# Graph attention layers on one core: the factors w spread by a transfer through DRAM, instead of by TensorE products

## The chip, the cores and the metric

The kernel runs on one core of a Trainium2 chip. The metric is the device time of one execution in microseconds (us); of several runs the median is taken. The engines are named as in the profile: PE is TensorE, DVE VectorE, ACT ScalarE, POOL GpSimd, SP SyncE, whose queue issues the transfers.

## The reference, cut to what matters

There are 64 graphs of 128 nodes with 384 features, and a 128 x 128 mask for each. Layer 0 is attention with 6 heads of 64, layer 1 graph attention with 12 heads of 32; both end in a residual sum and a layer norm. The change is in layer 1's weights:

```
h = einsum('bnd,ade->bane', feat_in, W);  th = tanh(h)
attn_src = einsum('bane,aeo->bano', th, w_src)
attn_dst = einsum('bane,aeo->bano', th, w_dst)
attn = attn_src + swapaxes(attn_dst, 2, 3)
attn = where(attn >= 0, attn, 0.2 * attn)
attn = softmax(where(~adj, -999.0, attn), axis=-1)
feat_out = einsum('banm,bame->bane', attn, h) + b
...
return gate * elu(feat_out) + (1.0 - gate) * feat_in
```

## The kernel before, in words

Work goes by groups of 4 graphs, 16 groups in all. Layer 1 of group u, layer 0 of group u+1 and the transposes of x for group u+2 are interleaved. Every engine has its program as a list of steps (name, graph or part k), in three tables: BEGIN, LOOP and END. LOOP is run 13 times as it stands, one pass per group. `phases` walks the tables, and `step` issues what a name stands for; so the order on each engine is fixed by hand-written tables, and semaphores make a step wait where its data or its buffer isn't there. Most buffers are doubled (k % 2). The products of 384 or 512 columns are made of three times three fp32r products of high and low parts (`project`, L573): ACT writes the high part (x1hi), DVE the low one (x1lo, L910).

In layer 1, the exponential of leaky(src_i + dst_j), divided by exp(src_i) (which the softmax cancels), is max(p_j, q_j w_i) with p = exp(dst), q = exp(0.2 dst), w = exp(-0.8 src). Node j lies on the partitions, i along them. The steps for one graph are:

- `h` (PE), `hout` (ACT, th at L836), `prod` (POOL, L1132), `sd`, `sda`, `wlog` (DVE, L1001 to L1012), then `pqw` (ACT): p, q and w as 128 x 12 each.
- `qwhi` and `qwlo` split q and w into parts (L866, L910), `qwT` transposes them (PE, L703) and `qwTo` copies them (ACT, L873).
- `rows` (POOL, L1139) lays w out as 96 x 1536 rows with zeros where the head is another's. `wb` (PE, three per graph, L712) multiplies: each gives q_j w_i for 4 heads as 128 x 512 in a PSUM bank, t_bank, of which there are two, shared with all transposes.
- `e` (DVE, L1032), three per graph with four instructions each, forms the weights of one head: the maximum with p_j and the minimum with clip, which holds the mask.
- `pv1` (PE, L726 and L732) sums values and denominators, `sumsTo`, `sumsT`, `rden1`, `f_raw`, `fb`, `elu`, `ex`, `mixa`, `mixb`, `sum1`, `stats1`, `mv1`, `rstd1` and `out` make y_out.

SP's program is short: per pass it issues the load of x_in and adj_in (`load`) and four stores. `maskT` and `clip` prepare the mask, `gate` and `gsum` the gate (L995), `x_res` (POOL, L1115) the residual with the biases.

## Time and profile before

| | us |
|---|---|
| median of 3 runs (1105.11 to 1106.05) | 1105.98 |
| profiled execution, its own time | 1105.45 |
| profiled execution, span | 1103.6 |
| PE busy | 1056.6 (96%) |
| DVE busy | 872.9 (79%) |
| POOL busy | 703.9 (64%) |
| ACT busy | 651.4 (59%) |

The busy shares are of the span. A pass of the loop repeats every 65.8 us from about 127 us on, 13 times. The drain (the last 120 us or so) holds what is left of the last two groups.

### The profile page before, as it was taken

The page shows a single profiled execution, that of the slowest core. Times are in us where ns is not written, and L with a number is a line of the kernel's source. Part 1 is how long each engine was busy: PE and PEld are TensorE (multiplying, and loading weights), DVE is VectorE, ACT ScalarE, POOL GpSimd, SP SyncE. Part 2 cuts the span into 40 slices and gives each one's busy share as a digit, 9 for nine tenths or more (in the row PEclk, how much of TensorE's full clock was granted, in tenths as well). Part 3 has the DMA queues.
Part 4 walks back from the last instruction along what each step waited for, and adds up shares of the span by engine and source line. Part 5 has one row for each costly group of instructions (what it writes and reads, how often), then busy time and mean ns, then how long its engine had stood idle before and what let it go on. Part 6 is the DMA issues. An engine that isn't in the chain of part 4 may idle for free.

```text
span 1103.6 us, 28424 instructions
## 1 busy us (share of the span) xinstructions
PE 1056.6 (96%) x9199; PEld 895.9 (81%) x9199; DVE 872.9 (79%) x2289; ACT 651.4 (59%) x2060; POOL 703.9 (64%) x605
## 2 busy tenths in 40 slices
PE   6999999999999999999999999999999999999964
PEld 4888888888888888888888888888888888888753
DVE  3659779696987969789696987969689796978986
ACT  4747466474755647565575746657565564747522
POOL 0347577575757758577574856757576674857764
PEclk9999999999999999999999999999999999999985
DMA  7101010010101001010100101001010100100000
...
DMA packets 34722, 31.00 MB, mean 28 GB/s; under 512 B 15872, under 2 KB 34688, under 8 KB 34688
## 3 DMA queue, kind: packets, MB, share of 16 engines
...
q14 instruction: 15, 0.12, 0.0%
...
## 4 chain that ended last, share of the span: by engine, by line
PE 79%; DVE 12%; issue 6%; ACT 1%; POOL 0%; DMA 0%; DVEq 0%; POOLq 0%; ACTq 0%
PE p_bank L573 50%; PE t_bank L712 5%; PE context L726 5%; DVE weights L1032 4%; PE scores L635 4%; PE context L732 4%; PE t_bank L644 3%; PE context L656 3%; PE t_bank L605 2%; PE t_bank L740 2%; PE t_bank L682 2%; DVE sd L1001 1%; DVE masked L940 1%; DVE neg_max L948 1%; PE t_bank L703 1%
## 5 line engine op out<-in xcount | busy, mean ns | idle before, releaser
L1139 POOL TENSOR_TENSOR w_rows<-qwT,own_head 96x1536 fp32r<-96x1536 f32 x64 | 179.8, 2810 | 87.0 <-ACT qwT L873 87.0
L1032 DVE SCALAR_TENSOR_TENSOR weights<-t_bank,pqw,clip 128x128 f32<-128x128 f32 x768 | 206.4, 344 | 7.4 <-PE t_bank L712 6.6
L1132 POOL TENSOR_TENSOR prod<-th,w_sd 128x768 f32<-128x768 f32 x64 | 118.2, 1846 | 124.8 <-ACT th L836 124.7
L808 ACT ACTIVATE probs<-masked,neg_max 128x128 f32<-128x128 f32 x384 | 148.8, 391 | 46.4 <-DVE neg_max L948 46.4
L573 PE MATMUL p_bank<-xT,w_q 128*128 128x512 f32 x432 | 113.6, 408 | 4.3 <-DVE w_k L917 4.3
L573 PE MATMUL p_bank<-w_v,xT 128*128 128x384 f32 x576 | 115.2, 344 | 1.2 <-DVE clip L985 1.2
L573 PE MATMUL p_bank<-w_f,cT 128*128 128x384 f32 x576 | 115.4, 344 | 0.4 <-DVE cT L910 0.4
L573 PE MATMUL p_bank<-w_h,x1T 128*128 128x384 f32 x576 | 114.0, 343 | 0.2 <-DVE x1T L910 0.2
L573 PE MATMUL p_bank<-w_g,x1T 128*128 128x384 f32 x576 | 113.9, 342 | 0.0
L573 PE MATMUL p_bank<-xT,w_k 128*128 128x512 f32 x432 | 111.5, 402 | 0.0
L1120 POOL TENSOR_TENSOR probs<-probs,rden 128x768 f32<-128x768 f32 x64 | 94.3, 1473 | 25.2 <-DVE rden L953 25.2
L573 PEld LDWEIGHTS p_bank<-w_h,x1T 128*128 128x128 f32 x576 | 101.7, 190 | 6.2 <-issue 2.6
L573 PEld LDWEIGHTS p_bank<-w_v,xT 128*128 128x128 f32 x576 | 99.7, 188 | 5.6 <-issue 3.6
L573 PEld LDWEIGHTS p_bank<-w_g,x1T 128*128 128x128 f32 x576 | 101.9, 190 | 2.1
L573 PEld LDWEIGHTS p_bank<-w_f,cT 128*128 128x128 f32 x576 | 99.1, 188 | 1.7 <-DVE cT L910 1.0
L573 PEld LDWEIGHTS p_bank<-xT,w_q 128*128 128x128 f32 x432 | 80.2, 191 | 24.4 <-DVE w_k L917 4.7
L1144 POOL TENSOR_TENSOR f_b<-f_raw,bias 128x384 f32<-128x384 f32 x64 | 71.3, 1113 | 42.0 <-DVE f_raw L1047 42.0
L1150 POOL TENSOR_TENSOR elu_steps<-elu_steps,x 128x384 f32<-128x384 f32 x64 | 75.0, 1172 | 31.0 <-ACT elu_steps L884 25.5
L1001 DVE TENSOR_REDUCE sd<-prod 128x24 f32<-128x768 f32 x64 | 60.4, 944 | 41.7 <-POOL prod L1132 41.7
L573 PEld LDWEIGHTS p_bank<-xT,w_k 128*128 128x128 f32 x432 | 79.5, 190 | 16.2
L712 PE MATMUL t_bank<-w_rows,qwT 96*128 96x512 f32 x192 | 84.1, 465 | 6.3 <-ACT probs0T L817 2.1
L995 DVE TENSOR_TENSOR gate_sum<-p_bank,gate_bias 128x384 f32<-128x384 f32 x64 | 35.1, 548 | 64.1 <-PE p_bank L573 64.0
...
## 6 DMA issues: line engine op xcount, KB each, us to landing
x_in<-in_x_dram SPq DMA_DIRECT2D x16, 768.0 KB, 4.7
out_dram<-y_out SPq DMA_DIRECT2D x64, 192.0 KB, 1.9
...
x<-in_L_gnn_W_dram SPq DMA_DIRECT2D x3, 192.0 KB, 6.1
```

What stands on the lines that cost most here:

```text
L573: last = te.matmul(dst, left(a, kt), right(b, kt), start=(n == 0), stop=(n == 3 * KT - 1))
L635: last = te.matmul(scores[:, b, j * P:(j + 1) * P], head(qT, j, b, k), head(kT, j, b, k), start=True, stop=True)
L712: te.matmul(dst[:, :], qwT[:, g % 2, 0, :], w_rows[0:QW_ROWS, g % 2, heads, :].rearrange("p h i -> p (h i)"), start=True, stop=True).then_ ...
L726: te.matmul(context1[t * HD1:(t + 1) * HD1, r * P:(r + 1) * P], h[:, k % 2, n * HD1:(n + 1) * HD1], weights[:, k % 2, n, :], start=(r == 0 ...
L808: last = act.activation(probs0[:, k % 2, b, j * P:(j + 1) * P], masked[:, k % 2, b * PAIRS + j, :], ACT.Exp, bias=neg_max[:, b * PAIRS + j ...
L1001: dve.tensor_reduce(sd[:].rearrange("p a h -> p (a h)"), prod[:].rearrange("p a (h e) -> p (a h) e", h=H1), AX_X, ALU.add).then_inc(s_sd, 1)
L1032: last = dve.scalar_tensor_tensor(out=weights[:, g % 2, n, :], in0=src[:, i * P:(i + 1) * P], scalar=pqw[:, g % 2, 0, n:n + 1], in1=clip[: ...
L1120: pool.tensor_tensor(probs, probs, per_head(rden0[:], P), ALU.mult).then_inc(s_norm, 1)
L1132: pool.tensor_tensor(prod[:], over_heads(th[:], 2), w_sd[:], ALU.mult).then_inc(s_prod, 1)
L1139: pool.tensor_tensor(w_rows[0:QW_ROWS, k % 2], over_heads(qwT[:, k % 2, 1, :].bitcast(F32), H1), per_head(own_head[:], P), ALU.mult).then_ ...
L1144: pool.tensor_tensor(f_b[:, k % 2, :].rearrange("p (h e) -> p h e", h=H1), f_raw[:].rearrange("p (h e) -> p h e", h=H1), over_heads(bias_1 ...
L1150: pool.tensor_tensor(exp_less_x, f_exp, x1[:, k, :], ALU.subtract).then_inc(s_ex, 1)
```

## The change

The products of w and q leave PE. Per graph:

- ACT's `pqw` writes p and q to a tile pq, and w to w_exp (128 x 12). `qwhi`, `qwlo`, `qwT`, `qwTo` and `wb` are gone, with their tiles.
- SP has two new steps. `keep` waits for w and writes it to a DRAM scratch w_kept (128 rows of 48 bytes). `spread` waits for that, and for the maxima that read the buffer two graphs before, and reads the 1536 numbers back to every partition: w_spread[:, k % 2] as [i, head], 768 KB.
- `rows` (POOL) now multiplies w_spread by q in place, 128 x 1536.
- `e` (DVE) reads head n of w_spread, every twelfth word, in place of a PSUM bank.
- SP now has tables of its own, and the tables of the four engines are new throughout.

The diff without the tables (one line of one table stands for them):

```diff
 PE_LOOP = [
-    ("v", 0), ("x1T", 0), ("qk", 0), ("x1T", 1), ("qk", 1), ("qk", 2), ("h", 0), ("gate", 0), ("qk", 3), ("h", 1),
+    ("qk", 0), ("qk", 1), ("x1T", 0), ("v", 0), ("qk", 2), ("x1T", 1), ("h", 0), ("gate", 0), ("x1T", 2), ("qk", 3),
...
+SP_LOOP = [
+    ("keep", 0), ("spread", 0), ("load", 0), ("keep", 1), ("spread", 1), ("keep", 2), ("spread", 2), ("keep", 3),
+    ("spread", 3), ("store", 0), ("store", 1), ("store", 2), ("store", 3),
+]
...
-        pqw = sb("pqw", [P, 2, 3, H1])
-        qw_parts = sb("qw_parts", [P, 2, 2, QW_ROWS], F32R)
-        qwT = sb("qwT", [QW_ROWS, 2, 2, P], F32R)
-        own_head = sb("own_head", [QW_ROWS, H1])
-        w_rows = sb("w_rows", [P, 2, H1, P], F32R)
+        pq = sb("pq", [P, 2, 2, H1])
+        w_exp = sb("w_exp", [P, 2, H1])
+        w_kept = [nc.dram_tensor(f"w_kept{i}", [P, H1], F32, kind="Internal").ap() for i in range(2)]
+        w_spread = sb("w_spread", [P, 2, P, H1])
...
+                elif name == "keep":
+                    sp.wait_ge(s_pqw, upto(g1, 3 * GROUP, 3 * k + 3))
...
+                    wait(sp, s_wspread[k % 2], upto(g1, GROUP // 2 * 16, k // 2 * 16))
...
+                    sp.dma_start(w_kept[k % 2], w_exp[:, k % 2, :]).then_inc(s_kept[k % 2], 16)
+                elif name == "spread":
+                    sp.wait_ge(s_kept[k % 2], upto(g1, GROUP // 2 * 16, (k // 2 + 1) * 16))
...
+                    wait(sp, s_e, upto(g1, THIRDS * GROUP, THIRDS * (k - 1)))
...
+                    sp.dma_start(w_spread[:, k % 2].rearrange("p i h -> p (i h)"),
+                                 w_kept[k % 2].rearrange("i h -> (i h)").partition_broadcast(P)
+                                 ).then_inc(s_wspread[k % 2], 16)
...
-                    te.matmul(dst[:, :], qwT[:, g % 2, 0, :],
-                              w_rows[0:QW_ROWS, g % 2, heads, :].rearrange("p h i -> p (h i)"),
-                              start=True, stop=True).then_inc(pe["wb"], 1)
...
+                    act.activation(w_exp[:, k % 2, :], wlog[:], ACT.Exp, scale=LEAKY - 1.0).then_inc(s_pqw, 1)
...
                     for i in range(H1 // THIRDS):
                         n = H1 // THIRDS * r + i
-                        last = dve.scalar_tensor_tensor(out=weights[:, g % 2, n, :], in0=src[:, i * P:(i + 1) * P],
-                                                        scalar=pqw[:, g % 2, 0, n:n + 1], in1=clip[:, g, :],
+                        last = dve.scalar_tensor_tensor(out=weights[:, g % 2, n, :], in0=w_spread[:, g % 2, :, n],
+                                                        scalar=pq[:, g % 2, 0, n:n + 1], in1=clip[:, g, :],
                                                         op0=ALU.max, op1=ALU.min)
...
                 elif name == "rows":
-                    pool.wait_ge(s_qwT, upto(g1, GROUP, k + 1))
...
-                    pool.tensor_tensor(w_rows[0:QW_ROWS, k % 2], over_heads(qwT[:, k % 2, 1, :].bitcast(F32), H1),
-                                       per_head(own_head[:], P), ALU.mult).then_inc(s_rows, 1)
+                    pool.wait_ge(s_wspread[k % 2], upto(g1, GROUP // 2 * 16, (k // 2 + 1) * 16))
+                    pool.wait_ge(s_pqw, upto(g1, 3 * GROUP, 3 * k + 2))
+                    pool.tensor_tensor(w_spread[:, k % 2], w_spread[:, k % 2], over_heads(pq[:, k % 2, 1, :], P),
+                                       ALU.mult).then_inc(s_prod1, 1)
```

How the tables move instructions is shown at three places. The first is PE in the loop, from the product of w_h with x1T of graph 0 on (names: w_h gives h, w_g the gate, w_q and w_k queries and keys). Before, and then in the change:

```order
L573 MATMUL p_bank<-w_h,x1T 128x384 x9
L463 REGISTER_ALU
L573 MATMUL p_bank<-w_g,x1T 128x384 x9
L573 MATMUL p_bank<-xT,w_k 128x512 x9
L573 MATMUL p_bank<-w_h,x1T 128x384 x9
L703 MATMUL t_bank<-ident,qw_parts 96x128 x2
L463 REGISTER_ALU
L573 MATMUL p_bank<-xT,w_q 128x512 x9
L679 REGISTER_ALU
L682 MATMUL t_bank<-ident,x 128x128 x3
```

```order
L582 MATMUL p_bank<-w_h,x1T 128x384 x9
L461 REGISTER_ALU
L582 MATMUL p_bank<-w_g,x1T 128x384 x9
L691 MATMUL t_bank<-ident,x 128x128 x3
L582 MATMUL p_bank<-xT,w_k 128x512 x9
L582 MATMUL p_bank<-w_h,x1T 128x384 x9
L461 REGISTER_ALU
L582 MATMUL p_bank<-xT,w_q 128x512 x9
L582 MATMUL p_bank<-xT,w_k 128x512 x9
L461 REGISTER_ALU
L582 MATMUL p_bank<-w_g,x1T 128x384 x9
```

Behind the gate of graph 0 there now stand the transposes of x1 for graph 2 and one product of 512 columns before h of graph 1, and two products of 512 columns before the gate of graph 1. The transposes of qw_parts are gone.

The second is DVE in the loop, at the maximum-minimum instructions of graph 0 (weights; masked and neg_max belong to layer 0 of the next group). Before, and then in the change:

```order
L948 TENSOR_REDUCE neg_max<-masked 128x6
L1022 REGISTER_ALU
L1032 SCALAR_TENSOR_TENSOR weights<-t_bank,pqw,clip 128x128 x8
L935 REGISTER_ALU
L940 TENSOR_TENSOR masked<-scores,neg 128x768
L1022 REGISTER_ALU
L1032 SCALAR_TENSOR_TENSOR weights<-t_bank,pqw,clip 128x128 x4
L1022 REGISTER_ALU
L1032 SCALAR_TENSOR_TENSOR weights<-t_bank,pqw,clip 128x128 x4
L1022 REGISTER_ALU
L1032 SCALAR_TENSOR_TENSOR weights<-t_bank,pqw,clip 128x128 x4
L953 RECIPROCAL rden<-den 128x6
```

```order
L910 REGISTER_ALU
L915 TENSOR_TENSOR masked<-scores,neg 128x768
L993 ISA
L461 REGISTER_ALU
L1000 SCALAR_TENSOR_TENSOR weights<-w_spread,pq,clip 128x128 x12
L923 TENSOR_REDUCE neg_max<-masked 128x6
L970 TENSOR_TENSOR gate_sum<-p_bank,gate_bias 128x384
L976 TENSOR_REDUCE sd<-prod 128x24
L928 RECIPROCAL rden<-den 128x6
L461 REGISTER_ALU
L983 TENSOR_TENSOR sda<-sd,sd_shift 128x24
L1000 SCALAR_TENSOR_TENSOR weights<-w_spread,pq,clip 128x128 x4
```

The twelve of graph 0 stood in pieces between two other steps, each waiting for a PSUM bank; now they stand in one piece after the second masked, and those of graph 1 follow after the sums sd of graph 2.

The third is SP in the loop, from its first DMA on. Before, and then in the change:

```order
L511 ISA
L511 DMA x_in<-in_x_dram 128x4x384
L512 REGISTER_ALU
L512 DMA adj_in<-in_adj_dram 128x4x128
L517 ISA
L518 ISA
L518 DMA out_dram<-y_out 128x384
L517 REGISTER_ALU
L518 ISA
L518 DMA out_dram<-y_out 128x384
```

```order
L520 DMA w_kept<-w_exp 128x12
L523 REGISTER_ALU
L461 REGISTER_ALU
L528 DMA w_spread<-w_kept 128x1536
L507 ISA
L511 ISA
L511 DMA x_in<-in_x_dram 128x4x384
L512 REGISTER_ALU
L512 DMA adj_in<-in_adj_dram 128x4x128
L515 REGISTER_ALU
L520 DMA w_kept<-w_exp 128x12
L528 DMA w_spread<-w_kept 128x1536
```

The load of x_in and adj_in now stands between the spread of graph 0 and the keep of graph 1; the stores follow behind the spread of graph 3.

## Rows read from the trace of the kernel before

**Rows 1.** The page: the span, then busy us (share) and instructions.

```profile
span 1103.6 us, 28424 instructions
...
PE 1056.6 (96%) x9199; PEld 895.9 (81%) x9199; DVE 872.9 (79%) x2289; ACT 651.4 (59%) x2060; POOL 703.9 (64%) x605
```

**Rows 2.** Windows: busy us in one middle pass and in the drain.

```profile
core 0: us, PE busy (x) PEld busy (x) DVE busy (x) ACT busy (x) POOL busy (x), PEclk, DMA share, GB/s
...
521.90:587.70 65.80, 65.11 (x575) 55.30 (x575) 53.66 (x143) 40.20 (x129) 44.00 (x38) 1.00 0.08 25
979.90:1103.60 123.70, 98.18 (x862) 81.37 (x861) 96.24 (x254) 55.73 (x176) 76.33 (x66) 0.88 0.05 19
```

**Rows 3.** PE in the middle pass: start us, us, instructions.

```profile
525.96 1.72 PE L573 MATMUL p_bank<-w_h,x1T 128*128 128x384 f32 x9
...
529.08 2.27 PE L573 MATMUL p_bank<-xT,w_k 128*128 128x512 f32 x9
...
532.81 0.42 PE L703 MATMUL t_bank<-ident,qw_parts 128*96 128x128 f32 x2
533.17 2.38 PE L573 MATMUL p_bank<-xT,w_q 128*128 128x512 f32 x9
...
542.77 0.39 PE L712 MATMUL t_bank<-w_rows,qwT 96*128 96x512 f32 x1
543.09 0.94 PE L635 MATMUL scores<-kT,qT 64*128 64x128 f32 x12
```

**Rows 4.** DVE in the same pass, same columns; in brackets the wait before.

```profile
524.14 0.56 DVE L910 TENSOR_TENSOR x1T<-t_bank,x1T 128x384 fp32r<-128x384 f32 x1
529.28 0.56 DVE L995 TENSOR_TENSOR gate_sum<-p_bank,gate_bias 128x384 f32<-128x384 f32 x1 [4.58 <-PE p_bank L573]
...
530.33 0.94 DVE L1001 TENSOR_REDUCE sd<-prod 128x24 f32<-128x768 f32 x1
...
542.62 0.94 DVE L948 TENSOR_REDUCE neg_max<-masked 128x6 f32<-128x768 f32 x1
543.48 2.15 DVE L1032 SCALAR_TENSOR_TENSOR weights<-t_bank,pqw,clip 128x128 f32<-128x128 f32 x8
...
546.40 3.19 DVE L1032 SCALAR_TENSOR_TENSOR weights<-t_bank,pqw,clip 128x128 f32<-128x128 f32 x12
549.50 0.19 DVE L953 RECIPROCAL rden<-den 128x6 f32<-128x6 f32 x1
...
577.85 0.55 DVE L1054 SCALAR_TENSOR_TENSOR mix<-f_b,elu_steps 128x384 f32<-128x384 f32 x1
578.31 0.23 DVE L1040 RECIPROCAL rden<-t_bank 128x12 f32<-128x12 f32 x1
```

**Rows 5.** Groups by line: busy us, mean ns | idle before, releaser.

```profile
L1132 POOL TENSOR_TENSOR prod<-th,w_sd 128x768 f32<-128x768 f32 x64 | 118.2, 1846 | 124.8 <-ACT th L836 124.7
...
L1115 POOL TENSOR_TENSOR x_res<-x_in,out_bias 128x1536 f32<-128x1536 f32 x16 | 56.0, 3499 | 28.2 <-DVE out_bias L925 28.2
...
L836 ACT ACTIVATE th<-p_bank 128x384 f32<-128x384 f32 x64 | 30.8, 481 | 19.0 <-PE p_bank L573 18.9
...
L910 DVE TENSOR_TENSOR qw_parts<-pqw,qw_parts 128x24 fp32r<-128x24 f32 x64 | 12.3, 193 | 26.9 <-ACT qw_parts L866 26.8
```

**Rows 6.** DMA issues of the page: count, KB each, median us to landing.

```profile
x_in<-in_x_dram SPq DMA_DIRECT2D x16, 768.0 KB, 4.7
out_dram<-y_out SPq DMA_DIRECT2D x64, 192.0 KB, 1.9
```

**Rows 7.** POOL in the middle pass, in order of time.

```profile
569.86 1.01 POOL L1150 TENSOR_TENSOR elu_steps<-elu_steps,x 128x384 f32<-128x384 f32 x1
...
575.85 1.63 POOL L1150 TENSOR_TENSOR elu_steps<-elu_steps,x 128x384 f32<-128x384 f32 x1 [1.34 <-ACT elu_steps L884]
```

**Rows 8.** PE in the drain, in order of time.

```profile
1062.58 0.90 PE L740 MATMUL t_bank<-ident,sumsT 128*128 128x128 f32 x4 [2.85 <-ACT sumsT L843]
...
1066.28 3.08 PE L573 MATMUL p_bank<-w_h,x1T 128*128 128x384 f32 x9
```

More of the change, by code:

```diff
@@ L187 @@
-    ("stats1", 2, 1), ("mixa", 3, 1), ("mixb", 3, 1), ("mv1", 2, 1), ("sum1", 3, 1), ("stats1", 3, 1), ("mv1", 3, 1),
-    ("out", 2, 1), ("out", 3, 1),
+    ("x1lo", 0, 0), ("gsum", 0, 0), ("x1lo", 1, 0), ("sd", 0, 0), ("sda", 0, 0), ("wlog", 0, 0), ("sd", 1, 0),
+    ("sda", 1, 0), ("wlog", 1, 0), ("gsum", 1, 0), ("x1lo", 2, 0), ("mask", 0, 0), ("max", 0, 0), ("e", 0, 0),
+    ("e", 1, 0), ("e", 2, 0), ("mask", 1, 0), ("rden0", 0, 0), ("max", 1, 0), ("x1lo", 3, 0), ("e", 3, 0),
+    ("e", 4, 0), ("e", 5, 0), ("sd", 2, 0), ("sda", 2, 0), ("wlog", 2, 0), ("rden1", 0, 0), ("f_raw", 0, 0),
@@ L217 @@
-ENGINES = ("PE", "ACT", "DVE", "POOL")
+    ("x_res", 0, 0), ("prod", 0, 0), ("prod", 1, 0), ("rows", 0, 0), ("rows", 1, 0), ("norm", 0, 0), ("prod", 2, 0),
+    ("fb", 0, 0), ("prod", 3, 0), ("norm", 1, 0), ("norm", 2, 0), ("ex", 0, 0), ("rows", 2, 0), ("norm", 3, 0),
+    ("fb", 1, 0), ("rstd0", 0, 0), ("ex", 1, 0), ("rows", 3, 0), ("rstd0", 1, 0), ("fb", 2, 0), ("prod", 0, 1),
+    ("rstd1", 0, 0), ("ex", 2, 0), ("prod", 1, 1), ("rstd0", 2, 0), ("rstd1", 1, 0), ("fb", 3, 0), ("rstd0", 3, 0),
@@ new lines @@
+    ("ex", 3, 0), ("rows", 0, 1), ("prod", 2, 1), ("rows", 1, 1), ("prod", 3, 1), ("rstd1", 2, 0), ("fb", 0, 1),
+    ("ex", 0, 1), ("rows", 2, 1), ("rstd1", 3, 0), ("rows", 3, 1), ("fb", 1, 1), ("ex", 1, 1), ("fb", 2, 1),
+    ("rstd1", 0, 1), ("ex", 2, 1), ("fb", 3, 1), ("rstd1", 1, 1), ("ex", 3, 1), ("rstd1", 2, 1), ("rstd1", 3, 1),
+]
+SP_BEGIN = [
+    ("load", 0, -1), ("keep", 0, 0), ("spread", 0, 0), ("keep", 1, 0), ("spread", 1, 0), ("keep", 2, 0),
+    ("load", 0, 0), ("spread", 2, 0), ("keep", 3, 0), ("spread", 3, 0), ("store", 0, 0), ("store", 1, 0),
+    ("store", 2, 0), ("store", 3, 0),
+]
@@ L218 @@
+ENGINES = ("PE", "ACT", "DVE", "POOL", "SP")
 ORDERS = {
-    "begin": dict(zip(ENGINES, (PE_BEGIN, ACT_BEGIN, DVE_BEGIN, POOL_BEGIN))),
+    "begin": dict(zip(ENGINES, (PE_BEGIN, ACT_BEGIN, DVE_BEGIN, POOL_BEGIN, SP_BEGIN))),
     "loop": {e: [(name, k, 0) for name, k in steps]
-             for e, steps in zip(ENGINES, (PE_LOOP, ACT_LOOP, DVE_LOOP, POOL_LOOP))},
-    "end": dict(zip(ENGINES, (PE_END, ACT_END, DVE_END, POOL_END))),
+             for e, steps in zip(ENGINES, (PE_LOOP, ACT_LOOP, DVE_LOOP, POOL_LOOP, SP_LOOP))},
+    "end": dict(zip(ENGINES, (PE_END, ACT_END, DVE_END, POOL_END, SP_END))),
@@ L514, in store @@
-            def store(t):
-                for g in range(GROUP):
-                    graph = at(t * GROUP + g)
-                    sp.wait_ge(s_y, upto(t, GROUP, g + 1))
-                    sp.dma_start(out_dram[:, bass.ds(graph, 1), :],
-                                 y_out[:, g % 2, :].unsqueeze(1)).then_inc(s_store[g % 2], 16)
-            load(1)
-            load(2)
-            store(0)
-            with sp.Fori(1, NG - 2) as u:
-                load(u + 2)
-                store(u)
@@ L529, in _ @@
+            phases(sp, step, "SP", NG)
             for g in range(2):
@@ L1155, in _ @@
             phases(pool, step, "POOL", NG)
-T_STAGES = {"sumsT", "pT", "qwT", "xT", "x1T", "wb", "maskT"}
+T_STAGES = {"sumsT", "pT", "xT", "x1T", "maskT"}
 P_STAGES = {"qk", "v", "f", "h", "gate"}
```

262 lines of the change are left out of this document (104 added, 158 removed), and 119 rows, old and new, of tables (DVE_BEGIN, DVE_END, DVE_LOOP, PE_BEGIN).

## The prediction

> **What bounds the kernel now.** I read the page's busy shares first, then the busy time of one pass of the loop, then PE's and DVE's instructions in that pass in order of time. It gives PE 96%, DVE 79%, POOL 64%, ACT 59% [rows 1]. These are means over start, 13 equal passes and drain, so the pass decides. In a middle pass of 65.80 us PE is busy 65.11 us at a granted clock of 1.00 (the 2.4 GHz level), DVE 53.66, POOL 44.00, ACT 40.20 [rows 2]. PE is the bound, but the other number to find is how far behind it DVE stands. DVE waits 65.80 - 53.66 = 12.1 us per pass. The first wait is the telling one: DVE makes the low part of x1T of a group's first graph at 524.14 (done 524.70), and the product that needs it starts on PE only at 525.96 [rows 3, 4]. So PE is ahead of DVE's need by 1.3 us, and all the rest of DVE's waiting, 10.8 us, is time in which DVE waits for work that it has itself let loose: DVE's own chain would give a pass of about 64.5 us. **There are two bounds, 65.8 and 64.5**, and a change that relieves PE alone is cut off 1.3 us down.
>
> **PE, relieved.** Out go 12 products t_bank<-w_rows,qwT and 4 pairs of transposes of qw_parts per pass. Their busy times overlap with their neighbours', so I take start to start: 542.77 to 543.09 is 0.32 us for a product, 532.81 to 533.17 is 0.36 for a pair [rows 3]. (12 x 0.32) + (4 x 0.36) = 5.3 us; PE's bound becomes 65.8 - 5.3 = 60.5 us.
>
> **ACT.** Three small copies per graph go from an engine that idles 25.6 us of the pass [rows 2]: nothing.
>
> **DVE, the term that decides.** Four small subtractions on qw_parts (193 ns each [rows 5], some 0.13 start to start) go: -0.5 us. The 48 maximum-minimum instructions stay, but their first operand moves from PSUM, 128 adjacent words, to SBUF, 128 words 12 apart (w_spread is laid out [i, head], and head n is read). Now: 12 of them from 546.40 to 549.50 are 0.258 us each [rows 4]. Without a price for the hop: two SBUF operands of 384 take 0.46 us start to start (577.85 to 578.31), and 768 read once take 0.86 (542.62 to 543.48), so a word costs 0.40/384 = 1.04 ns and 128 cost 0.46 - 256 x 1.04 ns = 0.19 us. No row shows DVE hopping. Bounds: hops free, 0.19 us (48 x -0.065 = -3.1 us); or as slow per word as the slowest elementwise row of the trace, GpSimd's x_res, 3499/1536 = 2.28 ns [rows 5], so 0.19 + 128 x 1.24 ns = 0.35 us (+4.5 us). I take twice the contiguous pace, 0.19 + 0.133 = 0.326 us (+3.3 us): every DVE row that fits 1.04 ns walks neighbours, and a walk that never uses a word's neighbour should not keep that pace. It is a choice, nearer to the upper end. DVE's work is then 53.66 - 0.5 + 3.3 = 56.5 us.
>
> The Trainium skill (Vector Engine (DVE) Microarchitecture Reference, section on rate slope and fixed cost, the SBUF access granule) says that a DVE port keeps its full rate only on runs of two or more adjacent words; it gives 1.73 ns per column for one source that hops far at every word, and 2.50 for both sources stepping 24 words. No run here shows it yet. By 1.73 the term would be +1.1 us, by 2.50 +5.9 us.
>
> **DVE's waits in the new order.** From the moment x1lo of graph 0 is done: PE runs h and gate, 525.96 to 529.08 [rows 3], so gate_sum starts 3.3 us later: a 3.3 us wait. gate_sum and x1lo 1 (529.28 to 530.33), sd, sda and wlog 0 (1.45 us) bring DVE to 5.8. Its next step, sd 1, needs h 1, which in the new PE order stands behind x1T 2 and one product of 512 columns: 3.12 + 0.25 + 2.1 + 1.7 = 7.2 (the 512 columns by the third row of [rows 3], 2.27 less the 0.16 that overlaps), then th 0.5 and prod 1.85 [rows 5], so 9.8: a wait of 4.0. sd, sda, wlog 1 to 11.25; gate 1 behind two more products of 512 columns ends at 13.1: 1.9. gate_sum, x1lo 2, masked 0, max 0 to 16.0; scores 1 ends at 16.4: 0.5. Sum 9.7 us that no speed of DVE shortens. Behind it DVE has 39 us of work in one stretch, where waits of POOL and ACT hardly show once DVE is the slow one: 0.5. **The pass is 56.5 + 9.7 + 0.5 = 66.7 us**, 0.9 more than now, with PE waiting 6 us in it.
>
> **The new transfer.** For the first graph: w_exp is ready 6.3 us after x1lo 0; a store of y_out lands in 1.9 us and an x_in of the same 768 KB as the spread in 4.7 [rows 6]; the product in place is x_res's case (1536 words, one operand repeated), 3.5 us. 6.3 + 1.9 + 4.7 + 3.5 = 16.4, and the first maximum-minimum stands at 17.4 (after masked 1). Hidden, with 1.0 us to spare. SP waits in the keep and in the spread; behind them stand the load, needed some 30 us later, and the stores, needed in the next pass: nothing. The bytes, 64 x 768 KB = 50 MB, are small beside idle queues (DMA share 0.08 [rows 2]). POOL's instruction stays one of 1536 words, and POOL idles 21.8 us of a pass [rows 2]: its length matters only where DVE waits for it. A GpSimd step can stretch, though: exp_less_x took 1.01 us beside maximum-minimum reading PSUM (569.86) and 1.63 beside DVE work on two SBUF operands (575.85) [rows 7]; the new one reads two SBUF operands, so the in-place product of graph 1 may take up to 5.6 instead of 3.5 us. It ends at 24 to 26 against DVE's need at 24: within the 0.5.
>
> The Trainium skill (GPSIMD Engine Reference, key points) names the contention of GpSimd with DVE instructions that have two SBUF inputs; these two rows agree with it (1.01 and 1.63 us).
>
> **Start and drain** hold three more groups. PE's saving there is up to 3 x 5.3 = 16 us where it bounds (at the start), DVE's loss 3 x 3.3 = 10 where that does (the last 123.7 us: DVE 96.2, PE 98.2 us busy at 0.88 [rows 2]); and the first and last chains are longer: 1.9 + 4.7 + 3.5 against about 4.6 us for copies, transposes, rows and product, +5.5 each. I take +3, between -10 and +11. **Sum:** the profiled execution took 1105.45 us (span 1103.6); 1105.5 + 13 x 0.9 + 3 = 1120.2. The median of the runs is 0.5 above it: 1121 us.
>
> **Rivals.** Hops are free (the other side: faster). The term is -3.1, DVE's work 50.1; the in-place products of graphs 1 and 3 and the exp chain then end 1 to 1.5 us after DVE is ready for each, 3.5 in all: 50.1 + 9.7 + 3.5 = 63.3, so 1105.5 - 13 x 2.5 - 3 = 1070. It decides at a start-to-start time below about 0.27 us. For it: DVE's writes of rden 4 words apart cost nothing that shows. Against: that is 12 words.
>
> Near steps cost more than twice. At a price above the GpSimd row, 0.38 us, the pass is 69.3 and the time 1105.5 + 46 + 6 = 1157. For it speaks no row, against it that not even GpSimd, at 2.28, is that slow on neighbours.
>
> The sentence of the Trainium skill's Vector Engine (DVE) Microarchitecture Reference on two sources at 24 words, 2.50 ns, is a rule that would bring this case about; our step is 12 words, on one source.
>
> The round trip is slow. If the 48-byte packets of the keep and the 128 reads of one row make it 3.2 us longer, the spare 1.0 is gone and each pass waits 2.2 us more at its first maximum-minimum, behind which all of DVE is queued: 1121 + 29 = 1150. For: no row shows packets of 48 bytes, nor one row read by all partitions in a quiet stretch; against: the two kinds shown agree with a small fixed time and 768 KB in 3 us more.
>
> PE's clock falls in the new wait. In a pass of 66.7 us PE has some 6 us to wait, and the order puts most of it at one place, before h of graph 0, behind DVE's x1lo. In the drain, after a wait of 2.85 us with little work around it, the nine products of w_h took 3.08 us instead of 1.72 (1.2 GHz, the granted clock 0.88 over the drain [rows 2, 8]). If each pass does the same, h and gate of graph 0 cost 3.1 us more, right on DVE's chain: 1121 + 13 x 3.1 = 1161. For: the drain; against: the drain has several waits in a row, here there is one in 66 us.
>
> PE stays the bound, which is what the counts of the diff alone suggest: 1105.5 - 13 x 5.3 = 1037, less if start and drain gain too. It needs DVE's 10 us of waits to vanish; the new order keeps them.
>
> **How the numbers follow.** Forecast (0.27 to 0.35 us per instruction, 1098 to 1135) 0.34; free hops 0.22; dearer hops 0.18; clock 0.12; slow round trip 0.08; PE bound 0.06. A measurement can tell 0.2%, some 2.2 us. Faster: 0.22 + 0.06 + 0.07 from the forecast's low edge = 0.35; same 0.06; slower 0.59. The range reaches down to take in free hops with their ends (1066), and up to the dear hops and the slow trip with half of the clock's case (1160).
>
> **What would show it.** Right: in a middle pass PE busy near 60 us of 66 to 67, DVE's long stretch without gaps, the maximum-minimum at 0.33 us start to start. Wrong: 0.19 to 0.25 there; or waits of DVE for w_spread's product at the first one; or transfers above 6 us. A pass near 60.5 would overturn the account of two bounds.

## The result, and the profile after

The changed kernel takes **1479.34 us** (median of 4 runs, 1476.95 to 1480.76), the kernel before in the same session 1105.55 us (1102.65 to 1106.05). The ratio is 1.3386, 95% interval 1.3355 to 1.3417: slower by a third. The forecast said slower, at 1121 us, and its range ended at 1160. The sign was right and the size was off by a factor of 24 (+374 us for +15.5). The terms that made it "slower" in the forecast come to 15 us, and the larger part of the 374 comes from one that stood there at next to nothing; so the right sign is in good part luck.

The page of the changed kernel, against [rows 1]:

```profile
span 1476.5 us, 27475 instructions
...
PE 1105.7 (75%) x8879; PEld 943.4 (64%) x8879; DVE 1221.2 (83%) x2225; ACT 611.3 (41%) x1868; POOL 749.6 (51%) x600
```

DVE has 64 instructions fewer than before and is busy 348 us longer (1221.2 against 872.9). That is nearly all of the loss, and the trace books it as *busy* time, not as idle time: something made DVE's instructions last. Two passes of the loop in the middle, against [rows 2] (windows: from:to, length, busy us of each engine, clock, DMA share, GB/s):

```profile
642.61:733.80 91.19, 69.65 (x554) 59.43 (x554) 76.17 (x139) 37.54 (x116) 46.60 (x37) 0.85 0.15 53
733.80:823.58 89.78, 68.44 (x554) 58.77 (x554) 76.07 (x139) 37.53 (x116) 46.69 (x37) 0.89 0.16 54
```

A pass went from 65.8 to 90.5 us, DVE in it from 53.7 to 76.1. Next the groups by line (mean ns of one behind the comma), for which [rows 5] stand; before, y_out had a mean of 483 ns, the first mix 551, the last sum 565:

```profile
L1000 DVE SCALAR_TENSOR_TENSOR weights<-w_spread,pq,clip 128x128 f32<-128x128 f32 x768 | 503.7, 722 | 3.7 <-POOL w_spread L1099 3.7
L1099 POOL TENSOR_TENSOR w_spread<-w_spread,pq 128x1536 f32<-128x1536 f32 x64 | 222.8, 3481 | 37.3 <-DMA w_spread<-w_kept 37.3
...
L1046 DVE TENSOR_SCALAR y_out<-sum,mv,rstd 128x384 f32<-128x384 f32 x64 | 74.9, 1170 | 1.7 <-POOL rstd L1065 0.7
...
L1022 DVE SCALAR_TENSOR_TENSOR mix<-f_b,elu_steps 128x384 f32<-128x384 f32 x64 | 54.4, 850 | 4.3 <-POOL elu_steps L1110 4.3
...
L1033 DVE SCALAR_TENSOR_TENSOR sum<-mix,x 128x384 f32<-128x384 f32 x64 | 46.8, 732 | 0.6
```

The maximum-minimum (called e below) has a mean of 722 ns, for 344 before. A mean hides what kind of loss it is, so the next view is the one line's own spread (minimum/median/maximum in ns), before and then in the change:

```profile
L1032 DVE SCALAR_TENSOR_TENSOR weights<-t_bank,pqw,clip x768: 311/343/354, 72.6 to 1086.0; 128x128 f32<-128x128 f32 x192
...
L1000 DVE SCALAR_TENSOR_TENSOR weights<-w_spread,pq,clip x768: 392/431/3522, 74.2 to 1460.0; 128x128 f32<-128x128 f32 x192
```

Median 431 ns, maximum 3522. So most of them pay a little (the hop, that is, the read of words 12 apart), and some take eight times the median. Before, none took over 354 ns. Where do the long ones stand? DVE's instructions in a stretch of the pass, in order of time (start us, us):

```profile
712.31 8.79 DVE L1000 SCALAR_TENSOR_TENSOR weights<-w_spread,pq,clip 128x128 f32<-128x128 f32 x12
...
746.99 7.64 DVE L1000 SCALAR_TENSOR_TENSOR weights<-w_spread,pq,clip 128x128 f32<-128x128 f32 x8
...
759.56 1.48 DVE L1000 SCALAR_TENSOR_TENSOR weights<-w_spread,pq,clip 128x128 f32<-128x128 f32 x4
760.95 0.56 DVE L1015 TENSOR_TENSOR f_raw<-t_bank,rden 128x384 f32<-128x384 f32 x1
...
778.78 3.60 DVE L1046 TENSOR_SCALAR y_out<-sum,mv,rstd 128x384 f32<-128x384 f32 x1
```

and POOL's in the same stretch:

```profile
713.90 1.91 POOL L1094 TENSOR_TENSOR prod<-th,w_sd 128x768 f32<-128x768 f32 x1 [2.61 <-ACT th L828]
715.77 3.46 POOL L1099 TENSOR_TENSOR w_spread<-w_spread,pq 128x1536 f32<-128x1536 f32 x1
...
747.14 1.52 POOL L1082 TENSOR_TENSOR probs<-probs,rden 128x768 f32<-128x768 f32 x1 [1.42 <-DVE rden L928]
748.63 1.03 POOL L1110 TENSOR_TENSOR elu_steps<-elu_steps,x 128x384 f32<-128x384 f32 x1
749.63 3.46 POOL L1099 TENSOR_TENSOR w_spread<-w_spread,pq 128x1536 f32<-128x1536 f32 x1
...
778.70 3.47 POOL L1077 TENSOR_TENSOR x_res<-x_in,out_bias 128x1536 f32<-128x1536 f32 x1
```

Where POOL idles, at 759.56, four e take 760.95 - 759.56 = 1.39 us, 0.35 each. Twelve e beside prod and the w_spread product take 8.79 us, which is 12 x 0.35 = 4.2 and another 4.6. And y_out, 0.08 us after x_res began, lasts until 0.21 us after x_res ended. The DVE instruction does not run slowly; it is held until the end of POOL's. All 172 e that last over 830 ns end 0.16 to 0.17 us after the end of a POOL instruction. That is less than an e's own 0.39, so it is let go a little before the end that is recorded for POOL.

Of 768 e 428 met no POOL instruction (longest 461 ns), 340 did (median 960; an overlap of over 50 ns counts). Before, 721 of the 768 lay beside a POOL instruction, and none lasted over 354 ns. In the changed kernel itself the lines of DVE that read PSUM, and the reductions and statistics with their one operand, keep their time too: gate_sum lasts 559 ns at most (median 550) with 38 of 64 beside POOL, the stats of layer 1 582 (550) with 49 of 64. Summed over all, e's time above its median is 228 us, of which 94 at the w_spread product and the rest at prod, probs, f_b and elu_steps; the rise of the median by 88 ns makes another 68. By the busy time of each group, e grew by 297 us (206.4 to 503.7), y_out by 44, mix by 19, sum by 11 and the x of layer 0 by 11 (475 to 626 ns); qw_parts' 12 us are gone, and sda, 24 words, lost 20 (533 to 218 ns). Together 350 us, against DVE's 348.

**Theories at this point.** Theory 1: an e that reads two buffers of SBUF and a POOL instruction exclude each other; before, e's first operand lay in PSUM. Theory 2: the read 12 words apart is the cost. Theory 3: the transfer through DRAM and the new orders make the passes long. DVE's idle time speaks against a large share of it: span less busy time is 231 us before and 255 in the changed kernel.

### The profile page after: what moved, and what is told of

Its sections match the earlier page's. It is cut to its first block, busy times and chain, and to the rows that moved or that the text cites. A ratio compares the mean times of both kernels' runs of the same rounds, so it can differ in the third digit from the quotient of the medians.

```text
span 1476.5 us, 27475 instructions
## 1 busy us (share of the span) xinstructions
PE 1105.7 (75%) x8879; PEld 943.4 (64%) x8879; DVE 1221.2 (83%) x2225; ACT 611.3 (41%) x1868; POOL 749.6 (51%) x600
## 4 chain that ended last, share of the span: by engine, by line
DVE 32%; issue 29%; PE 27%; POOL 9%; ACT 1%; DMA 1%; DVEq 1%; POOLq 0%; ACTq 0%; SPq 0%
PE p_bank L582 18%; DVE weights L1000 17%; POOL w_spread L1099 3%; PE context L718 2%; POOL prod L1094 2%; DVE mix L1022 2%; PE context L724 2%; PE scores L644 2%; DVE sum L1033 2%; PE t_bank L732 1%; POOL f_b L1104 1%; DVE sd L976 1%; DVE f_raw L1015 1%; DVE stats L1037 1%; PE t_bank L653 1%
## 5 line engine op out<-in xcount | busy, mean ns | idle before, releaser
L1000 DVE SCALAR_TENSOR_TENSOR weights<-w_spread,pq,clip 128x128 f32<-128x128 f32 x768 | 503.7, 722 | 3.7 <-POOL w_spread L1099 3.7
L718 PE MATMUL context<-weights,h 128*32 128x128 f32 x1536 | 108.8, 367 | 256.2 <-DVE weights L1000 256.2
L1099 POOL TENSOR_TENSOR w_spread<-w_spread,pq 128x1536 f32<-128x1536 f32 x64 | 222.8, 3481 | 37.3 <-DMA w_spread<-w_kept 37.3
L718 PEld LDWEIGHTS context<-weights,h 128*32 128x32 f32 x1536 | 55.6, 143 | 275.5 <-DVE weights L1000 272.8
L582 PE MATMUL p_bank<-w_h,x1T 128*128 128x384 f32 x576 | 134.9, 386 | 46.9 <-DVE x1T L885 46.5
L582 PE MATMUL p_bank<-w_g,x1T 128*128 128x384 f32 x576 | 129.2, 375 | 4.2 <-DVE gate_sum L970 4.2
L582 PEld LDWEIGHTS p_bank<-w_g,x1T 128*128 128x128 f32 x576 | 115.3, 215 | 7.8 <-issue 4.9
L830 ACT ACTIVATE h<-p_bank 128x384 f32<-128x384 f32 x64 | 31.2, 488 | 208.0 <-PE context L724 208.0
L724 PE MATMUL context<-weights,one_hot 128*32 128x128 f32 x1536 | 110.4, 372 | 0.0
L835 ACT ACTIVATE sumsT<-context 128x512 f32<-128x512 f32 x64 | 38.0, 593 | 150.3 <-PE context L724 150.3
```

Of the source, the lines that this page charges most:

```text
L582: last = te.matmul(dst, left(a, kt), right(b, kt), start=(n == 0), stop=(n == 3 * KT - 1))
L718: te.matmul(context1[t * HD1:(t + 1) * HD1, r * P:(r + 1) * P], h[:, k % 2, n * HD1:(n + 1) * HD1], weights[:, k % 2, n, :], start=(r == 0 ...
L724: last = te.matmul(context1[t * HD1:(t + 1) * HD1, D:D + P], one_hot[:, r, :], weights[:, k % 2, n, :], start=False, stop=(r == THIRDS - 1))
L835: act.activation(sumsT[:], context1[:, :], ACT.Copy).then_inc(s_sumsT, 1)
L1000: last = dve.scalar_tensor_tensor(out=weights[:, g % 2, n, :], in0=w_spread[:, g % 2, :, n], scalar=pq[:, g % 2, 0, n:n + 1], in1=clip[:, ...
L1099: pool.tensor_tensor(w_spread[:, k % 2], w_spread[:, k % 2], over_heads(pq[:, k % 2, 1, :], P), ALU.mult).then_inc(s_prod1, 1)
```

## The experiments

Where no ratio is given, the time is that of a single execution. The kernel before took 1106.45 us beside adjacent, pool_short, one_operand and old_adjacent, 1104.3 (median) beside adj_short, old_hop, split4 and act_spread, and 1105.1 beside one_short, act_adjacent and fold_act; its times spread by 0.5%.

### One part of the new operand at a time

**e reads adjacent words** (label adjacent):

```diff
- in0=w_spread[:, g % 2, :, n],
+ in0=w_spread[:, g % 2].rearrange("p i h -> p (i h)")[:, n * P:(n + 1) * P],
```

> The changed kernel with one edit: the weights step e reads 128 adjacent words of w_spread in place of 128 words 12 apart. The pairs' factors are then the wrong ones (left out: that word (i, h) goes with pair (i, h)); the amount of work of every instruction is the same. Theory 1 (two buffers of SBUF: a VectorE instruction whose two data operands both lie in SBUF does not finish while a GpSimd instruction runs; it waits that one out): only the hop's price goes, about 0.15 us x 48 = 7 us in a pass of 90.5, so about 1380 us, and some of the e instructions beside w_spread still last 1 to 3.5 us. Theory 2 (the read 12 apart is itself what costs, by a cost that varies with what else reads SBUF): e falls to 0.19 to 0.26 us for all, and the kernel to about 1110 us. Theory 3 (the transfer and the new orders make the passes long, not e): within 30 us of 1479.

Measured: 1403.47 us, 76 less than the changed kernel, where theory 1 had said about 1380.

```profile
L1000 DVE SCALAR_TENSOR_TENSOR weights<-w_spread,pq,clip x768: 300/342/3568, 75.6 to 1385.0; 128x128 f32<-128x128 f32 x192
```

The median falls from 431 to 342 ns, what it was with PSUM (343), and the maximum stays. The hop costs 89 ns of 128 words, 0.70 ns a word, the same for each. Theory 2 asked for 1110: it falls. The hop is a part (76 us), and not the large one. Theory 1's value was too low since it took the hop at 150 ns.

**POOL's product cut to 12 words** (label pool_short):

```diff
- pool.tensor_tensor(w_spread[:, k % 2], w_spread[:, k % 2], over_heads(pq[:, k % 2, 1, :], P),
+ pool.tensor_tensor(w_spread[:, k % 2, 0:1], w_spread[:, k % 2, 0:1], over_heads(pq[:, k % 2, 1, :], 1),
```

> The changed kernel with one edit: GpSimd multiplies 12 of the 1536 words of each partition of w_spread by q (left out: q in the other 1524, so layer 1's weights lack q). Every other instruction, buffer and wait stays. Theory 1 (VectorE waits out a running GpSimd instruction): GpSimd's 3.48 us x 4 per pass go, and with them the e that last up to 3.5 us; what is left are x_res and prod, so 13 to 20 us less per pass, 1200 to 1310 us. Theory 2 (the read 12 apart costs by itself): e stays at 0.72 us mean, and the kernel within 20 us of 1479, since GpSimd was at work only half of the time. Theory 3 (the transfer is late): the product leaves the path from the transfer to e, 3.4 us sooner per group, at most 7 us per pass: not under 1390.

Measured: 1356.95 us, 122 less. e itself is untouched, POOL was idle half of the time, and DVE's e are busy 93 us less (410.6 for 503.7). Their longest is now 1930 ns, a prod long, where it was a w_spread product long. The effect was smaller than my 1200 to 1310: of the 228 us only the 94 at the product are gone, and the 133 at prod, probs (`norm` in the tables), f_b and elu_steps are still there, 133 us.

**Both together** (label adj_short):

> The changed kernel with two of the edits of the first batch together: e reads 128 adjacent words, and GpSimd multiplies 12 words of each partition (left out: q in the others, and the right pairing of w's words). Alone they gave 1403 (-76) and 1357 (-122). If they are one loss counted twice (an e that is shorter meets fewer GpSimd instructions, and fewer GpSimd instructions leave less to meet), the two together give less than their sum: 1290 to 1320. If they add up as independent costs: 1281. What then remains over 1106 is e beside prod, norm and x_res, and y_out beside x_res: by the kernel before with a plain SBUF operand (1307) not below 1250.

Measured: 1297.82 us, -182 for -76 and -122: a little less than the sum, and in the range for one loss that is partly counted twice. What remains over the kernel before is 193 us, with a plain read and hardly a product.

**e with one SBUF operand** (label one_operand):

```diff
- last = dve.scalar_tensor_tensor(out=weights[:, g % 2, n, :], in0=w_spread[:, g % 2, :, n],
-                                 scalar=pq[:, g % 2, 0, n:n + 1], in1=clip[:, g, :],
-                                 op0=ALU.max, op1=ALU.min)
+ last = dve.tensor_reduce(weights[:, g % 2, n, :], w_spread[:, g % 2, :, n:n + 1], AX_X, ALU.max)
```

> The changed kernel with one edit: e becomes a VectorE reduction over one element with the same 128 words 12 apart read and the same 128 bf16 written, so it reads one SBUF buffer, not two (left out: the max with p and the min with the clip; layer 1's weights are w q alone, also where there is no edge). GpSimd's product stays whole. Theory 1 (two SBUF buffers are what makes it wait for GpSimd): no e lasts over 0.5 us, beside w_spread or not, and the e part of the loss (about 235 of 373 us) goes: 1200 to 1270 us, y_out and mix still stretched. Theory 2 (the read 12 apart costs by itself): unchanged, 1479 within 30. Theory 3 (transfer and orders): unchanged.

Measured: 1241.65 us, 238 less, with the hop, the transfer, the long product and all orders in place.

```profile
L1000 DVE TENSOR_REDUCE weights<-w_spread x768: 296/375/406, 75.5 to 1223.5; 128x128 f32<-128x128 f32 x192
```

None is over 406 ns, though 532 of the 768 now lie beside a POOL instruction. So neither the hop nor the buffer that POOL works on too makes an e wait. The edit also changes the kind of instruction, so that it is the second operand in SBUF rests on this run together with old_adjacent below, which changes nothing but the place of an operand. The profile shows at once who is next in the queue. The first mix, with two SBUF operands, now meets the products and goes from 850 to

```profile
L1020 DVE SCALAR_TENSOR_TENSOR mix<-f_b,elu_steps 128x384 f32<-128x384 f32 x64 | 96.7, 1511 | 4.2 <-POOL elu_steps L1108 4.2
```

**That and the short product** (label one_short), for the 136 us which that kernel still has over the one before:

> The changed kernel with two edits of the first batch together: e is a reduction with one SBUF operand, and GpSimd multiplies 12 words per partition (left out: the max with p, the min with the clip, and q in most words). Alone they gave 1242 and 1357. Theory 1: with the one e meets nobody, so what is left of 136 us over the kernel before is mix, sum and y_out beside GpSimd; without the 3.48 us products mix falls from 1.51 back to 0.7 us and sum stays at 0.6 to 0.76, which is 50 to 60 us less: 1175 to 1200 us, y_out beside x_res (45 us) being left. If instead the 136 us are the new orders and the way through DRAM, the product's length matters little: 1225 to 1242 us.

Measured: 1175.91 us, 66 less, at the lower edge. Left are 71 us, and DVE is busy 69 us longer than before (942.0 for 872.9): y_out beside x_res (1170 for 483 ns, 64 times: 44 us), mix (964 for 551: 26 us), sum (679 for 565: 7 us) and e (375 for 344 ns: 26 us), less sda and qw_parts (35 us). DVE's idle time is 232 us, for 231 before. So nothing of size is left over for the transfer or for the orders as such: theory 3 falls. What the new orders do is to place y_out beside x_res and mix beside POOL's work.

### The cost brought into the kernel before

**e's operand in SBUF, nothing else changed** (label old_adjacent):

```diff
- last = dve.scalar_tensor_tensor(out=weights[:, g % 2, n, :], in0=src[:, i * P:(i + 1) * P],
+ last = dve.scalar_tensor_tensor(out=weights[:, g % 2, n, :], in0=w["f"][:].bitcast(F32).rearrange("p a k n -> p (a k n)")[:, 0:P],
```

> The kernel before with one edit: e's first operand is 128 adjacent words of a constant buffer in SBUF in place of the products' bank of PSUM (left out: layer 1's factors w q; all transposes and products on TensorE still run, and all waits stay). No DRAM transfer, no GpSimd product, no read 12 apart, old orders. Theory 1 (two SBUF buffers wait out GpSimd): slower than before although the read is plain: e instructions of 1 to 3.5 us appear beside x_res, prod and norm, which fill 44% of the middle pass; some 10 us per pass, 1180 to 1280 us. Theory 2 (only the read 12 apart costs): not slower than 1106, 1060 to 1106 us since SBUF is read at least as fast as PSUM. Theory 3 (transfer and orders): 1106 within 20.

Measured: 1306.89 us, 200 more than the kernel before and above my 1180 to 1280, for one operand's place. No scratch, no new orders, no hop, and POOL does what it always did. e's spread went from 311/343/354 to

```profile
L1032 DVE SCALAR_TENSOR_TENSOR weights<-w_f,pqw,clip x768: 303/341/5973, 71.7 to 1289.3; 128x128 f32<-128x128 f32 x192
```

5973 ns is longer than any POOL instruction. The four e around one of them on DVE, and POOL beside it:

```profile
710.53 6.76 DVE L1032 SCALAR_TENSOR_TENSOR weights<-w_f,pqw,clip 128x128 f32<-128x128 f32 x4
```

```profile
710.23 2.75 POOL L1139 TENSOR_TENSOR w_rows<-qwT,own_head 96x1536 fp32r<-96x1536 f32 x1 [3.10 <-ACT qwT L873]
712.94 3.41 POOL L1115 TENSOR_TENSOR x_res<-x_in,out_bias 128x1536 f32<-128x1536 f32 x1
```

w_rows ended at 712.98 and x_res had begun at 712.94; the waiting e did not get its turn in between, and was held until x_res was done. 27 of the 768 were passed over so, 14 of them for over 3.6 us. My range had no such case.

**The same, 12 apart** (label old_hop; the slice is [:, n:n + 12 * P:12]):

> The kernel before, as in the run on 128 adjacent words of a constant SBUF buffer (1306.9 us), now with 128 words 12 apart of that buffer (left out again: the factors w q). Theory 1: an e that meets no GpSimd instruction takes 0.43 us in place of 0.34, which is 48 x 0.09 = 4.3 us of work per pass, and longer e meet GpSimd more often: 60 to 100 us over 1307, so 1370 to 1410. If the hop were the large cost and the two SBUF buffers a small one, it would have to be over 1479.

Measured: 1362.66 us, +56: a little under my 60 to 100. For one e the hop costs nearly the same in both kernels, 86 ns here (median 427 for 341) and 89 there; in time it is 56 us here and 76 there, and why is not shown.

### Does a shorter POOL instruction help?

**The product in four pieces** (label split4):

```diff
- pool.tensor_tensor(w_spread[:, k % 2], w_spread[:, k % 2], over_heads(pq[:, k % 2, 1, :], P),
-                    ALU.mult).then_inc(s_prod1, 1)
+ for part in range(4):
+     rows = slice(P // 4 * part, P // 4 * (part + 1))
+     last = pool.tensor_tensor(w_spread[:, k % 2, rows], w_spread[:, k % 2, rows],
+                               over_heads(pq[:, k % 2, 1, :], P // 4), ALU.mult)
+ last.then_inc(s_prod1, 1)
```

> The changed kernel with one edit: GpSimd's product w_spread times q is issued as four instructions of 128x384 words, back to back, in place of one of 128x1536; the results are the same. Theory 1a (VectorE waits for the end of the GpSimd instruction that runs, and gets its turn before the next): an e that met the 3.48 us product waits at most 0.9 us for a piece, so the e over 1.3 us beside w_spread are gone; e's busy time falls from 504 towards 420 us, and the kernel by 50 to 100 us, to 1380 to 1430. Theory 1b (VectorE waits until GpSimd pauses, so it doesn't get in between back-to-back instructions, as the e of 5.97 us in the last batch, which lay beside w_rows and x_res one behind the other, suggests): e still lasts up to 3.5 us or more, and the kernel is within 15 us of 1479 or slower by the pieces' own start-up. Theory 2 (the read 12 apart costs by itself): no change, within 15 us.

Measured (4 executions): 1463.08 us, ratio to the kernel before 1.3253 (1.3220 to 1.3287), so about 1% under the changed kernel. Theory 1a's picture was right and its price wrong. The line's spread, and twelve e on DVE with the four pieces on POOL:

```profile
L1000 DVE SCALAR_TENSOR_TENSOR weights<-w_spread,pq,clip x768: 395/435/1915, 73.8 to 1444.2; 128x128 f32<-128x128 f32 x192
...
701.74 8.44 DVE L1000 SCALAR_TENSOR_TENSOR weights<-w_spread,pq,clip 128x128 f32<-128x128 f32 x12
...
705.35 3.99 POOL L1101 TENSOR_TENSOR w_spread<-w_spread,pq 128x384 f32<-128x384 f32 x4
```

The longest e is now a prod long, so DVE does get in between the pieces. But it gets one e in per piece: the four e beside these four pieces last 1.08 to 1.17 us, while the pieces go on at 0.99 to 1.04 us each. 251 of the 768 e last over 1 us, where 159 did, and e's waits at the product fall from 94 us only to 78. What has to shrink is the time for which POOL is busy where e runs, not the length of one instruction.

### Is there a better kernel in it?

If two SBUF operands are the cost, w may come through DRAM as long as it lies in PSUM when e reads it. **ScalarE puts it there, times q** (label act_spread; TensorE only gives the bank, the orders are those of the kernel before without its steps for qw):

```diff
+ for i in range(H1 // THIRDS):
+     n = H1 // THIRDS * r + i
+     last = act.activation(t_bank[t_at("wb", k, turn)][:, i * P:(i + 1) * P],
+                           w_spread[:, g % 2, :, n], ACT.Copy, scale=pq[:, g % 2, 1, n:n + 1])
```

> A third way, from the theory that two SBUF operands are what costs: w still goes through the DRAM scratch and lies spread in SBUF, but ScalarE reads it 12 apart, scales it by q (the activation's per-partition scale) and writes four heads at a time into a bank of t_bank in PSUM, where the products of the kernel before lay; e reads them there, adjacent, with one SBUF operand, as before. TensorE's products and transposes of w and q, GpSimd's w_rows and the product on GpSimd are gone. The orders are those of the kernel before. Theory 1: no e is over 0.36 us, VectorE's work is that of before less 0.8 us per pass, TensorE's less 5.3, GpSimd's less 11.3, ScalarE's plus 48 x 0.2 to 0.3 less 4, so about 8: to 49 of 65.8. VectorE stays the bound: 1060 to 1110 us, my value 1090. Theory 2 or 3 (the transfer or the read 12 apart costs): ScalarE's copies are late, and e waits for them: over 1150.

Measured (4 executions): 1303.32 us, ratio 1.1799 (1.1771 to 1.1827). My number was 1090; the half of theory 1 that speaks of DVE's e holds, ScalarE's part was mis-sized.

```profile
L1059 DVE SCALAR_TENSOR_TENSOR weights<-t_bank,pq,clip 128x128 f32<-128x128 f32 x768 | 216.0, 344 | 207.7 <-ACT t_bank L907 207.5
L907 ACT ACTIVATE t_bank<-w_spread,pq 128x128 f32<-128x128 f32 x768 | 326.0, 474 | 30.9 <-PEq L754 16.2
```

e is back at 344 ns, and waits 208 us for ACT, whose copy takes 474 ns and not the 0.2 to 0.3 us that I had priced. How much of that is the hop is seen in **the same with adjacent reads** (label act_adjacent):

> The kernel in which ScalarE scales w by q into PSUM (1303 us), with its source read as 128 adjacent words in place of 128 words 12 apart (left out: that the words go with the right pair). If ScalarE's 0.474 us is the hop's, as VectorE's e pays 0.09 us for it, the instruction falls to 0.22 to 0.35 us and the kernel to 1150 to 1230 us; if it is the size of a scaled copy into PSUM, it stays at 0.47 us and 1303 us.

Measured: 1231.36 us; the copy takes 354 ns, both just over the ranges. So the hop costs ScalarE 120 ns of 128 words (0.94 ns a word). Against the middle of the 0.2 to 0.3 us priced above, the miss of 0.22 is half the hop and half the instruction itself.

**q folded into h, one copy for four heads** (label fold_act): e becomes min(max(w, p/q), clip), GpSimd multiplies h by q in place, and the sums' columns of ones become columns of q.

```diff
- w_kept = [nc.dram_tensor(f"w_kept{i}", [P, H1], F32, kind="Internal").ap() for i in range(2)]
+ w_kept = [nc.dram_tensor(f"w_kept{i}", [H1, P], F32, kind="Internal").ap() for i in range(2)]
+ last = act.activation(t_bank[t_at("wb", k, turn)][:],
+                       w_spread[:, g % 2, heads, :].rearrange("p h i -> p (h i)"), ACT.Copy)
```

> The kernel in which ScalarE puts w into PSUM (1303 us) with its cost taken down. w goes to the DRAM scratch head by head, so that it lies adjacent in SBUF after the spread; ScalarE copies four heads, 512 words, with one instruction; q leaves e: e is min(max(w, p/q), clip), GpSimd multiplies h by q (128x384, in place), and the columns of ones for the sums become columns of q, written by the activation that makes q. GpSimd's w_rows, TensorE's products and transposes of w and q, and DVE's split of q stay gone. From the rows: ScalarE's sumsT copy of 512 words is 0.59 us, so 12 x 0.59 = 7.1 us per pass for 48 x 0.47 = 22.8; ScalarE is then at about 45 of 65.8 us, GpSimd at 44 - 11.3 + 4.3 = 37, VectorE at 53, TensorE at 60. Theory 1 (two SBUF operands beside GpSimd): e 0.34 us, no longer than before; 1050 to 1110 us, my value 1080. Theory 3 (the way through DRAM is late in itself): e waits for ScalarE, which waits for the transfer; over 1150.

Measured (6 executions): 1665.03 us, ratio 1.5082 (1.5054 to 1.5111), the worst of all. It came out as theory 3 had said, with the way through DRAM late, but by what this edit had done to that way. SP's queue, in order of time:

```profile
727.99 0.37 SPq L573 DMA_DIRECT2D w_kept<-w_exp  x1
738.75 0.34 SPq L582 DMA_DIRECT2D w_spread<-w_kept  x1
```

The second waits for the first to land: 10.8 us from issue to issue for 6 KB, written in 1536 pieces of 4 bytes. I had changed the layout of the scratch to save ScalarE the hop, and given no price to the writes.

**The scratch laid out as before, ScalarE hops** (label fold_hop):

> The kernel with q folded into h and the sums' columns (1665 us), with the scratch laid out again as the changed kernel's (12 words of a node side by side, 128 writes of 48 bytes in place of 1536 of 4 bytes); ScalarE hops while it copies: four heads, 512 words 12 apart, with one instruction. In the trace of the last run the way into the scratch took 10.7 us (728.0 to 738.7) where the changed kernel's takes 1.5, and the wait for it 679 us of the queue's time. Theory: that store alone is what went wrong, so the time drops below the 1231 us of the kernel with adjacent scaled copies, whose ScalarE works 48 x 0.354 = 17.0 us per pass at this, to my 12 x (0.59 + 512 x 0.94 ns) = 12.9 us: 1130 to 1220 us, my value 1180. To beat the kernel before (1105) it would have to be hidden wholly, and e's wait for ScalarE at 134 us in that kernel speaks against it. Rival: the folding itself costs (h times q on GpSimd lies between h and the context products): over 1231.

Measured (5 executions): 1221.46 us, ratio 1.1058 (1.1037 to 1.1078), 1.5 us above the range. The store's price was what made the 1665: only the scratch's layout and the way ScalarE reads it are changed, and the second of these costs time. The hopping copy of 512 words takes 1078 ns, as worked out (0.59 + 0.48 = 1.07); e still waits 117 us for it. No version with the way through DRAM came under the kernel before.

## Why the prediction was wrong, step by step

**What failed** is the paragraph on the new transfer, its last step: that a POOL instruction "can stretch", by 0.6 us, "within the 0.5" of the pass. I had read in [rows 7] that POOL's instruction is the one that suffers. The rows show only who came second. When exp_less_x (1.63 us) started at 575.85, DVE was on x (a TENSOR_SCALAR from SBUF to SBUF, 575.66 to 576.13), with the sum of mix and x, two SBUF operands, behind it to 576.61; its 1.01 us of work end at 577.48, so it was held until about 576.47. A DVE instruction that starts while POOL runs is held as well, and POOL's are 1 to 3.5 us long, not 0.5. The change made 48 more instructions per pass of the kind that can lose, beside a POOL busy for 47 us of the pass. e then added 297 us for the forecast's 68 ns x 768 = 52, and y_out, mix, sum and x another 85. In the sum, the term is DVE's work of a pass: 76.2 us, where 56.5 stood.

The trace of the kernel before had it, in the spread of one small DVE line, sda (24 words, two SBUF operands), and in order of time:

```profile
L1008 DVE TENSOR_TENSOR sda<-sd,sd_shift x64: 167/185/1643, 63.8 to 1072.9; 128x24 f32<-128x24 f32 x64
...
536.55 1.64 DVE L1008 TENSOR_TENSOR sda<-sd,sd_shift 128x24 f32<-128x24 f32 x1
```

Median 185 ns, longest 1643, which ends at 538.19, 0.05 us after the w_rows that POOL had begun at 535.38 (2.76 us). wlog, a TENSOR_SCALAR of 12 words from SBUF to SBUF, has a longest of 2746 ns there, with a median of 174. The minimum, median and maximum of DVE's lines would have shown it before the change was made.

The Trainium skill states this rule (SBUF — State Buffer, "Who interferes with whom" and "SBUF: two separate sides"): DVE's second SBUF port pair is GpSimd's only one, and it is an exclusive lock. A DVE instruction with two SBUF inputs contends for it with a GpSimd instruction that reads SBUF, one in a two-port mode with any; whoever starts first has it for the whole instruction, and the other waits. The runs agree: e with two SBUF operands lasts up to 3522 ns in the changed kernel, with one at most 413 (one_short). y_out, 3.60 us beside x_res, has one data operand; by the page it would have to be in a two-port mode, and no run here shows its mode. The prediction named only a short line of another page, that there is contention, and took a size for it from one row.

**The hop** was priced at 0.326 us start to start, between 0.19 and 0.35. Measured 0.35 (1.39 / 4), the upper end. Both parts were wrong, and came near by luck: I had put two adjacent SBUF operands at 0.19 us, and they take what PSUM takes (342 ns against 343, and 0.26 start to start in both); the hop adds 0.09, and I had put 0.13. The Vector Engine (DVE) Microarchitecture Reference of the Trainium skill ("Measured stream behaviour on trn2", the SBUF access granule) has 1.73 ns per column where one source hops 4 KiB at every word. Our step of 48 bytes comes to the same: 1.04 + 0.70 = 1.74 ns.

**The waits of DVE's chain** were worked out as 3.3, 4.0, 1.9 and 0.5 us. The trace has them at these places (the wait in brackets):

```profile
698.12 0.56 DVE L970 TENSOR_TENSOR gate_sum<-p_bank,gate_bias 128x384 f32<-128x384 f32 x1 [6.22 <-PE p_bank L582]
...
705.05 0.95 DVE L976 TENSOR_REDUCE sd<-prod 128x24 f32<-128x768 f32 x1 [4.41 <-POOL prod L1094]
...
707.91 0.56 DVE L970 TENSOR_TENSOR gate_sum<-p_bank,gate_bias 128x384 f32<-128x384 f32 x1 [1.39 <-PE p_bank L582]
...
711.43 0.96 DVE L915 TENSOR_TENSOR masked<-scores,neg 128x768 f32<-128x768 f32 x1 [0.52 <-PE scores L644]
```

Three are met within 0.5 us. The first is 2.9 us longer in this pass, and that is what **the rival on PE's clock** had named, at the place where it was put:

```profile
691.96 3.25 PE L582 MATMUL p_bank<-w_h,x1T 128*128 128x384 f32 x9 [3.48 <-DVE x1T L885]
695.00 3.08 PE L582 MATMUL p_bank<-w_g,x1T 128*128 128x384 f32 x9
...
706.15 1.73 PE L582 MATMUL p_bank<-w_g,x1T 128*128 128x384 f32 x9
```

After a wait of 3.48 us for DVE, h and gate of graph 0 run at half the pace (3.08 for 1.73): the granted clock is 0.50 to 0.52 from 692.0 to 698.1, 1.2 GHz, and 1.00 behind it, 2.4 GHz. But the wait comes from the same exclusion, since the y_out in front of x1T lasted 3.55 us for its 0.47: without it some 0.4 us of PE's 3.48 would be left, by these rows. No run has the new orders without the long y_out, so whether the clock would have fallen without it is not shown. The wait of DVE is 6.2 us in every other pass and 5.05 in those between, so some 31 us over the forecast's 3.3 in all; the share in the 374 was not tried by itself. The granted clock of the whole run rises as the runs get shorter: 0.870 in the changed kernel, 0.891, 0.910 and 0.949 in adjacent, pool_short and one_operand.

**The transfer** was hidden, as forecast: the keep lands in 1.5 us and the spread in 4.0 (1.9 and 4.7 taken), and e waits for w_spread's product 3.7 us in the whole run. **PE** as the bound (1037) was out: it is busy 69.7 of 91.2 us, more than the 60 that I had expected, with the clock granted at 0.85. Of DVE's time in the first of the two windows, 76.2 us are work and 15.0 waits. So of the 24.5 us that the sum of 66.7 lacks, 19.7 are DVE's work and 4.8 its waits.

**The range** failed since its ends were made of the hop's price, a slow trip and half of the clock's case, and none of its cases had two engines that take turns.
